# A two-layer convolution network on parity grids: convolutions in 64x64 pieces of the array, two row tiles at a time

## The reference

```python
def odefunc(t, y):
    h = jax.nn.relu(_group_norm(y, gn1_w, gn1_b))
    h = _concat_conv(t, h, conv1_w, conv1_b)      # 3x3, pad 1, an input channel of the constant t in front
    h = jax.nn.relu(_group_norm(h, gn2_w, gn2_b))
    h = _concat_conv(t, h, conv2_w, conv2_b)
    return _group_norm(h, gn3_w, gn3_b)

x = x + dct2(_gn(x))                              # 2-D DCT of each 112x112 channel
y = _gn(x)
for k in range(6): y = y + (1/6) * odefunc(k/6, y)
return x + y                                      # x: 16 images, 32 channels, 112 x 112, float32
```

## Time and profile before

| | |
|---|---|
| median of 3 runs | 3935.17 us (3934.33 to 3935.84) |
| profiled execution, its span | 3928.6 us |
| PE busy, share of the span | 3592.0 us, 91% |
| PEld | 2039.1 us, 52% |
| DVE | 3342.3 us, 85% |
| ACT | 2079.6 us, 53% |
| POOL | 929.9 us, 24% |
| mean granted clock of TensorE | 0.970 |

### The profile page before, as it was taken

One profiled execution on the slowest core, in us unless ns is written; L12 is line 12 of the kernel. 1 busy time (PEld: TensorE's weight loads), 2 busy tenths in 40 slices (PEclk: granted clock), 3 DMA queues, 4 the chain that ended last, 5 costly groups with the idle time before them and its releaser, 6 DMA issues.

```text
span 3928.6 us, 70526 instructions
## 1 busy us (share of the span) xinstructions
PE 3592.0 (91%) x21844; PEld 2039.1 (52%) x21844; DVE 3342.3 (85%) x7423; ACT 2079.6 (53%) x3169; POOL 929.9 (24%) x1589
## 2 busy tenths in 40 slices
PE   3699999999999999999999999999999999999995
PEld 3455554555555555555555555555555555554553
DVE  7688888888888888888888888888888888888885
ACT  0455565555655556555565545655555555655553
POOL 4022212222122221222212231123211322111211
PEclk7899999999999999999999999999999999999998
DMA  3300033113032130311312113311133112231013
GB/s 79 74 17 16 22 45 84 41 60 70 11 84 62 61 58 10 94 63 41 58 42 83 41 41 58 76 49 41 41 58 84 41 41 62 37 83 49 25 41 99
DMA packets 366284, 210.26 MB, mean 54 GB/s; under 512 B 351104, under 2 KB 351472, under 8 KB 364016
## 3 DMA queue, kind: packets, MB, share of 16 engines
q1 hardware_dynamic: 366064, 207.66, 21.2%
HBM read 104.88 MB, written 77.07 MB: 46 GB/s over the span
## 4 chain that ended last, share of the span: by engine, by line
issue 39%; PE 34%; DVE 14%; POOL 10%; ACT 2%; POOLq 1%; DMA 1%; DVEq 0%; SPq 0%; ACTq 0%
PE cps L1246 30%; POOL xn L516 3%; POOL small L479 3%; DVE hb L973 2%; POOL m L513 2%; POOL xn L521 2%; PE xps L1320 2%; DVE hb L976 2%; ACT z L620 2%; DVE bnt L889 1%; POOL hb L496 1%; DVE bnt L896 1%; DVE small L951 1%; DVE bn L1000 1%; DVE ha L976 1%
## 5 line engine op out<-in xcount | busy, mean ns | idle before, releaser
L1246 PE MATMUL cps<-ha,w 128*128 128x399 f16 (+1 forms) x9216 | 1737.6, 342 | 69.7 <-DVE ha L976 64.5
L1246 PE MATMUL cps<-hb,w 128*128 128x448 f16 x8064 | 1645.0, 360 | 0.0
L608 ACT ACTIVATE z<-cps,bias_now 128x448 f32<-128x448 f32 (+2 forms) x1440 | 875.8, 610 | 1128.3 <-PE cps L1246 1100.9
L1246 PEld LDWEIGHTS cps<-ha,w 128*128 128x128 f16 x9216 | 861.0, 99 | 693.6 <-ACT z L608 61.1
L1246 PEld LDWEIGHTS cps<-hb,w 128*128 128x128 f16 x8064 | 748.9, 100 | 678.8 <-issue 41.5
L479 POOL TENSOR_TENSOR small<-small,half 128x1 f32<-128x1 f32 x304 | 190.3, 626 | 2135.6 <-DVE small L942 2133.8
L496 POOL MEMSET hb<- 64x28 f16 (+2 forms) x1152 | 320.5, 278 | 784.6 <-DVE hb L976 666.2
L889 DVE BATCH_NORM_STATS2 bnt<-z 128x6 f32<-128x448 f32 x672 | 413.1, 621 | 94.7 <-ACT z L608 94.7
L620 ACT ACTIVATE z<-z,small 128x798 f32<-128x798 f32 (+1 forms) x384 | 405.8, 1057 | 120.5 <-DVE small L951 120.5
L982 DVE SCALAR_TENSOR_TENSOR y<-z,small,y 128x784 f32<-128x784 f32 x384 | 457.4, 1245 | 6.7
L896 DVE BATCH_NORM_STATS2 bnt<-z 128x6 f32<-128x385 f32 (+1 forms) x768 | 411.4, 546 | 56.9 <-ACT z L608 50.4
(11 more groups left out here) (135 smaller groups left out, 2352.4 us busy)
## 6 DMA issues: line engine op xcount, KB each, us to landing
xa<-x_dram SPq DMA_DIRECT2D x64, 392.0 KB, 7.9
y<-xa SPq DMA_DIRECT2D x16, 1568.0 KB, 7.7
y_dram<-y SPq DMA_DIRECT2D x64, 392.0 KB, 7.1
xs<-in_x_dram SPq DMA_DIRECT2D x31, 784.0 KB, 8.7
x_dram<-x1s SPq DMA_DIRECT2D x30, 784.0 KB, 5.3
fin<-y_dram SPq DMA_DIRECT2D x30, 784.0 KB, 7.8
fin<-x_dram SPq DMA_DIRECT2D x28, 784.0 KB, 8.3
out_dram<-fin SPq DMA_DIRECT2D x28, 784.0 KB, 3.3
```

What stands on the lines that cost most here:

```text
L608: nc.scalar.activation(z[slot][:, r0 * width:(r0 + r) * width], cps[i % BANKS][:, 0:r * width], ACT.Identity, bias=bias_now[:, conv:conv + ...
L1246: return pe.matmul(ps, w[:, tap, wl, :], h[:, hl, r0 + a:r0 + a + r, b:b + width], start=(n == 0), stop=(n == len(products) - 1))
```

## The change

The column parities are no longer shifted between the convolutions: both keep 56 columns, while rows still go from 56 to 57 and back. For columns a 3x3 kernel then has one tap between equal parities and two between different ones (`taps`). Partitions 0 to 63 hold one column parity and 64 to 127 the other, and each product becomes a 64x64 piece from one half of the partitions (`hin`) to one half of the outputs (`hout`).

A pair of row tiles, P from rows of the upper half and Q from rows 28 further down, is convolved together. For rows 28 to 55 the state is stored with its column parities swapped. So the pieces that cross parities in P run between other halves than those of Q, and a round has four pieces on four different quarters of the array, with two banks. X phases have 12 rounds, Y phases 6; `PHASES` orders the four pairs of a convolution. Six banks (three pairs) are used, and the rims' products are 64x64 pieces too.

- ScalarE evacuates pairs of 784 elements per partition (`evacuate`), 4 instead of 7 or 8, with an extra row in convolution 1; it writes the hi part of the hb split itself by a second activation (`activate`); it normalises the half image for the DCT in 16 instructions (`normalise_half`) and copies the rim weights of the step (`set_bias`).
- VectorE loses the hb casts and the rim statistics, takes statistics of 392 elements (`pair_stats`), and takes over `last_add`.
- GpSimd loses `zero_rim`, `centre_half`, `scale_half` and `last_add`. It gets `wrap_rows` (copies the first row of hb to below the last, and zeroes the first, two partition ranges) and `seam` (copies two rows of ha between halves where the swap lies).
- The orders of ScalarE, VectorE and TensorE's small products are written anew for four pairs per phase. Weights shrink to three column taps; state loads and stores go in eight DMAs of half the size instead of four.

```diff
-                products = [(tap, wl, hl) for wl, hl in ((0, 0), (0, 1), (1, 0)) for tap in range(4)]
-                    return pe.matmul(ps, w[:, tap, wl, :], h[:, hl, r0 + a:r0 + a + r, b:b + width],
-                                     start=(n == 0), stop=(n == len(products) - 1))
+PHASES = (("X", 0), ("X", 1), ("Y", 0), ("X", 2), ("Y", 1), ("X", 3), ("Y", 2), ("Y", 3))
+PAIR_BANKS = ((0, 1, 2, 0), (1, 2, 0, 1), (2, 0, 1, 2), (2, 0, 1, 2))
+                taps = {(0, 0): ((1, 0),), (1, 1): ((1, 0),), (1, 0): ((0, -1), (2, 0)), (0, 1): ((0, 0), (2, 1))}
+                def piece(at, first, rows, idx, hin, hout, ix, ox, n):
+                    kinds = [(wl, hl, tap, a) for wl, hl in ((0, 0), (0, 1), (1, 0)) for tap in taps[ix, ox]
+                             for a in range(2)]
+                    wl, hl, (kx, dj), a = kinds[n]
+                    off = (first + idx + a) * P + 1 + dj
+                    src = h[hin * 64:(hin + 1) * 64, hl, off:off + rows * P].rearrange("p (i j) -> p i j", j=P)
+                    dst = cps[hout * 64:(hout + 1) * 64, at:at + rows * NA].rearrange("p (i j) -> p i j", j=NA)
+                    return pe.matmul(dst, w[hin * 64:(hin + 1) * 64, kx, a, wl, :], src[:, :, 0:NA],
+                                     start=(what == "X" and n == 0), stop=(what == "Y" and n == len(kinds) - 1))
+                rounds = 12 if what == "X" else 6
+                for n in range(rounds):
+                    if n in between:
+                        between[n]()
+                    if n == 0:
+                        ready()
...
+                    if what == "X":
+                        p_piece(1, 0, n)
+                        p_piece(0, 1, n)
+                        q_piece(0, 0, n)
+                        last = q_piece(1, 1, n)
+                    else:
+                        p_piece(0, 0, n)
+                        p_piece(1, 1, n)
+                        q_piece(1, 0, n)
+                        last = q_piece(0, 1, n)
```

TensorE, a step's small products (phases 0 to 3; a place is a phase of `PHASES` and a round):

```diff
+                between = {(1, 6): lambda: statistics_of(Z1, 0)}
...
+                between = {(1, 6): lambda: statistics_of(Z1, 1)}
...
+                between = {(1, 6): lambda: statistics_of(Z2, 0)}
...
+                elif kind != LAST:
+                    between[7, 0] = lambda: statistics_of(Y, 0)
...
+                between = {(0, 0): lambda: statistics_of(Z2, 1)}
+                if kind == MID:
+                    for b in range(2):
+                        between[1 + 2 * b, 0] = lambda b=b: rows_of(b)
+                        between[2 + 2 * b, 0] = lambda b=b: dct_columns(b, NBATCH * hn + b, dps)
+                    def state_then_rows():
+                        statistics_of(Y, 1)
+                        rows_of(2)
+                    between[5, 0] = state_then_rows
```

ScalarE, phases 0 and 1, and phase 2:

```diff
+                    evacuate(slot, conv, phase, 0, c)
+                    act.wait_ge(post_done, posted(Z1, other))
+                    activate(other, Z1, 0)
+                    activate(other, Z1, 1)
+                    evacuate(slot, conv, phase, 1, c)
+                    activate(other, Z1, 2)
+                    evacuate(slot, conv, phase, 2, c)
+                    activate(other, Z1, 3)
+                    evacuate(slot, conv, phase, 3, c)
...
+                if kind == MID:
+                    normalise_half(hn)
+                evacuate(1, 1, 2, 0, c)
...
+                    squares(0, 0)
+                    squares(0, 1)
+                    evacuate(1, 1, 2, 1, c)
+                    squares(0, 2)
+                    squares(0, 3)
+                    evacuate(1, 1, 2, 2, c)
+                    evacuate(1, 1, 2, 3, c)
+                    act.wait_ge(post_done, posted(Y, 0))
+                    for k in range(NP):
+                        activate(0, Y, k)
```

VectorE, phase 2 and the start of phase 3 (`updated` waits for the statistics, aggregates, gets the coefficients and updates the state; in phase 3 a split part stands between aggregation and coefficients):

```diff
+                    split_for(3, 0)
+                    split_for(3, 1)
+                    stats_of(2, 2)
+                    stats_of(2, 3)
...
+                updated(1, 1, lambda: split_for(3, 3))
```

More of the change, by code:

```diff
@@ L577, in _ @@
+                seam(0, conv_at(g, s, 3), fixes + 2, pows)
+                pows = rsqrt_of(Z2, 1)
+                if kind != FIVE:
+                    pows = rsqrt_of(Y, 1)
+                seam(1, conv_at(g, s, 4), fixes + 3, pows)
+                if kind == FOUR:
+                    rsqrt_of(IZ, 0)
             with pool.Fori(0, GROUPS - 1) as g:
@@ new lines, in step @@
+                split_for(2, 0)
+                split_for(2, 1)
+                stats_of(1, 1)
+                if kind == MID:
+                    half_post(hn, stats_before(g, s, kind) + STATS[MID].index((X0, 0)))
+                split_for(2, 2)
+                if kind == FIVE:
+                    post_of(IY, 0)
+                if kind == FOUR:
+                    start_stats(0, g + 1, (0, 1))
+                split_for(2, 3)
+                if kind == MID:
+                    with dve.If(g > 0):
+                        last_add(g * HALVES + s)
@@ L1267, in needs, with pair_tiles @@
-            def needs(conv, k):
-                rows = (TILES1, TILES2)[conv]
-                parts = (PARTS_A, PARTS_B)[conv]
-                last = offsets(rows)[k] + rows[k] + (0 if conv == 0 else 1)
-                last = min(last, sum(parts))
-                return next(p + 1 for p in range(NP) if offsets(parts)[p] + parts[p] >= last)
-            def tile(slot, conv, k, i, n, t, ready, base, between=()):
-                if k == 0 or needs(conv, k) > needs(conv, k - 1):
-                    pe.wait_ge(ready, base + needs(conv, k))
-                if not (isinstance(n, int) and n + i < BANKS):
-                    pe.wait_ge(evac_done, n + i - BANKS + 1)
-                conv_tile(slot, conv, k, i, t, between)
+            def pair_tiles(conv, k):
+                if conv == 0:
+                    first = (0, R + 1) if k == 0 else (R * k + 1, R)
+                    return (*first, R * k + 1 + HALF, R, 1)
+                return (R * k, R, R * k + HALF, R, 0)
@@ L1367, in statistics_of @@
                     statistics(slot, what, stats_before(g, s, kind) + STATS[kind].index((what, slot)), wait, value)
-                def among(*places):
-                    return {(k, m): (lambda e=event: statistics_of(*e)) for k, m, event in places}
-                i = 8
-                between = among((2, {MID: 1, FOUR: 1, FIVE: 10}.get(kind, 6), (Z1, 0)))
-                if kind == FIVE:
-                    between.update(among((7, 0, (IZ, 1))))
-                for k in range(8):
-                    tile(1, 0, k, i, n, s, lo_done, parts - NP, between)
-                    i += 1
@@ L1383, in step @@
+                between = {(1, 6): lambda: statistics_of(Z1, 1)}
                 if kind == MID:
[L1384 removed]
+                    between[3, 0] = lambda: half_mean(hn, stats_before(g, s, kind) + STATS[MID].index((X0, 0)))
                 if kind == FIVE:
[L1386 to L1389 removed]
@@ L1391, in step @@
-                between = among((1, 9 if kind == FIVE else 3, (Z2, 0)))
-                if kind not in (FIVE, LAST):
-                    between.update(among((4, 9, (Y, 0))))
-                elif kind == FIVE:
-                    between.update(among((4, 0, (IY, 1))))
-                for k in range(7):
-                    tile(1, 1, k, i, n, s, rim_zero, rim + NP, between)
-                    i += 1
+                    between[5, 0] = lambda: statistics_of(IY, 0)
+                convolve(0, 1, 1, conv_at(g, s, 1), sets + 1, between)
```

920 lines of the change are left out of this document (510 added, 410 removed).

## The result

The changed kernel takes 4397.7 us (median; 4391.8 to 4404.2), the kernel before 3935.5 us beside it: ratio 1.117, 95% interval 1.116 to 1.119. It is 11.7% slower, where 7% faster was forecast; 4398 lies above the range that I gave (3440 to 4120), too.

What follows compares the result with a forecast made beforehand. With no engine full any more, queue order was taken to decide: start 172, seven groups 3066, last group 370, tail 34 make 3642, plus 6.6 outside the span: 3650 us, 7% below; range 3440 to 4120.

Steps and rivals of the forecast that it cites:

- Rounds of 170 ns, loads hidden: TensorE's convolutions: four 64x64 pieces run together in 170 ns, their four weight loads hidden under the stream.
- weight loads queue: Slower rival, between a round's pieces: four loads queue, 225 ns per round, 4055 us in all; chance 0.28.
- less overlap: Slower rival: pieces run in twos, 340 ns a round, TensorE bound again, sum 5350 us; chance 0.16.
- TensorE's part of the sum: Each convolution: 72 rounds of 0.170 us plus 0.8 us of rims, 13.1 us instead of 16.8.
- VectorE 59 us, ScalarE about 54 us in a MID step: Work per step with a half image's DCT: VectorE 59 us, ScalarE about 54 us instead of 42.4.
- The standing behind GpSimd: VectorE operations slowed beside GpSimd's long passes: about 8 us per MID step, expected to go.
- The walk: Queue orders followed through one MID step's four phases, stalls included: 75.5 us.
- eight DCT batches: TensorE's DCT products in a MID step: eight batches at 0.8 us, 6.4 us, as in the kernel before.
- 43.4: no stall: Phase 2: squares end at 43.0 us, the state's product stands at 43.4, so TensorE waits 0.
- evacuation of the last pair 4 to 5 us after its pieces: Sign of being right: ScalarE evacuates a convolution's last pair 4 to 5 us after TensorE finishes it.
- The clock: TensorE products at half clock after the stalls in phase 1 and ahead of phase 3: 1.7 us each.
- FOUR and FIVE: The two steps of each group after its four MID steps: 70 us and 66 us.

Runs made afterwards that it cites:

- b1_nopool: Kernel before, with GpSimd's centring and scaling of the half image moved to ScalarE and its last add to VectorE: 3833.8 us, ratio 0.974.
- e10_flat: Changed kernel with TensorE's loops over the MID steps of a group and over the last group's steps written out: 4329.2 us, ratio 1.100.
- e2_fill: Changed kernel with idle 64x64 pieces on TensorE, read by nobody, ahead of three statistics products of each step: 4155.0 us, ratio 1.056.
- e1_late: Changed kernel with the small statistics products placed later between TensorE's pieces, nothing else: 4298.2 us, ratio 1.093.
- e4_order: e1_late with phase 3's product later still and VectorE's split parts, last add and statistics in another order: 4044.9 us, ratio 1.028.
- e6_all: e4_order with the sixteen normalisations split into two parts and the second hb activation taken back to a VectorE cast: 4006.1 us, ratio 1.018.
- e8_fill: e6_all with idle 64x64 pieces on TensorE in three of its waits: 3922.5 us, ratio 0.995.
- e11_fillflat: e8_fill with TensorE's loops over MID steps written out: 3806.6 us, ratio 0.968.
- e12_best: e11_fillflat with image 1's squares together, its state's product earlier, and eight normalisations ahead of phase 2's squares: 3800.8 us, ratio 0.966.

## Why the prediction was wrong, step by step

*Rounds of 170 ns, loads hidden*: right. 169 ns is the median. The loads of four different quarters do not add up. The rivals "weight loads queue" and "less overlap" fall, although the first named a time (4055) nearer to the one measured. TensorE's part of the sum, 13.1 us a convolution, holds: phase 0 in the step shown (1601.4 to 1617.5) takes 16.1 us with a wait of 2.9 in it.

*VectorE 59 us, ScalarE about 54 us in a MID step*: right, 59.45 and 53.05, the second with some luck: its terms as written add up to 50 to 53 us, and the sixteen normalisations were taken at 0.25 us; they took 0.38 from start to start (6.05 for sixteen) and 0.47 each. The line through 448 and 798 columns did not hold at 112. The last add, 1.8: 1.78. The standing behind GpSimd, 8 us: b1_nopool shows 8.5.

*The walk*: this is where it failed. The terms of a MID step, forecast against measured:

| term | forecast | kernel after |
|---|---|---|
| wait at the product of phase 1 | 3.7 | 5.0 |
| wait at the product of phase 2 | 0 | 5.1 |
| wait ahead of phase 3 | 7.6 | 8.0 |
| wait in phase 0 for split part 2 | 0 | 2.9 |
| rounds at half clock | 3.4 | 5.0 in 31 rounds; 5.7 with those that hold rim pieces |
| eight DCT batches | 6.4 | 7.7 |
| jump back, three MID steps of four | 0 | 2.5 in the mean, by e10_flat |

The measured waits are from piece to piece. Added up, they miss by 15 to 16 us, and the gap between 75.5 and 91.5 (mean of four) is 16.0. Over the span: the start took 189.7 instead of 172, 18 us more; the seven groups 3721.6 (189.7 to 3911.3) instead of 7 x 438 = 3066, 656 more; what follows them 490.7 instead of 370 + 34, 87 more. Their sum, 760, is the span of 4402.0 less the 3642 forecast for it; from median to forecast it is 748.

The row of the DCT had its cause in the change too. From the first of eight products to the next convolution piece it is 0.97 us in the kernel after (median of 196 batches), between 64x64 pieces, and 0.79 before (224 batches), between 128x128 products; the two small statistics products take 0.31 instead of 0.14 us. I had carried the old price over for the first and had none for the second. Timeline of TensorE at full clock:

```profile
1598.18 1.04 PE L1477 MATMUL dps<-dct,xn 112*112 112x112 f32 x8
1599.15 0.53 PE L1369 MATMUL cps<-ha,w 64*64 64x392 f16 x8
```

The step that failed is "43.4: no stall". I had walked the coefficients of phase 2 to the updates and squares, and asked only whether the state's product would wait. But the statistics product of the same chain stands at (1, 6), three us into phase 2, and I had evacuation 3 at 33.1 against a start of 31: even by my own numbers it would have waited about 1 us. Read from the trace, the other 4 are three: evacuation 3 ended 3.5 us into the phase instead of 2.1; the last add, which I had costed at 1.8 us and put into a sum, stands ahead of these very statistics (1551.52 against 1553.22 above); and the statistics of both last pairs stand behind it, 1.97 us where I had walked one pair's. No run moves the last add alone. This wait, 5.1 us where the walk has 0, is the largest single miss of a MID step, a third of the 16. The same with phase 0: split part 2, counted in the sum, stands behind the aggregation (aggregation 1604.00, subtraction 1605.17 to 1606.15, TensorE's next piece 1606.49). Sum and walk used the same terms, but in the walk I had queued them only on ScalarE.

And a wait that I had not thought of as such feeds itself: while TensorE stands, evacuation 0 of the next convolution, which ScalarE has in its queue ahead of the activations, cannot run. In phase 1 the coefficients were there at 1538.1, ScalarE idled 8.4 us in all and took evacuation 0 at 1540.54, the activations behind it at 1541.35. The prediction's last check, "evacuation of the last pair 4 to 5 us after its pieces", looked at the wrong end of that queue.

*The clock*: the mechanism was there, the size was not. Two waits with 1.7 us of slow products behind each, 3.4 us; there were three with slow rounds behind them, 31 in the MID step shown, and a fourth wait, 2.9 us, without. e2_fill puts a price on it, 243 us of the kernel's 4398.

*The jump*: no term at all. It is 69 us of the kernel after, 116 where little else waits.

The shares, as the runs show them one after the other (in another order they would be others: the clock was worth 243 us first and 84 later): order of TensorE's and VectorE's queues 353 us (e1_late, e4_order), hb cast and normalising 39 (e6_all against e4_order; 109 for the cast alone on the kernel after), clock 84 on top of that (e8_fill), jump 116 (e11_fillflat), the rest of the order 6, inside the noise. Together 597 of 748. In the mean e12_best's MID steps take 77.2 us, 1.7 above the forecast's 75.5 (46 us in all), its steps of the last group 69.9 (8 us). FOUR and FIVE, 75.8 and 71.7 against 70 and 66, are 80 us of what is left, the start 15. FOUR stays open: its chain was never walked, only set by a few words, and no run bears on it. Of FIVE the traces show more. Behind it stands the jump back of the whole group, which no run wrote out. Timeline of TensorE in e12_best, at the start of the fourth group:

```profile
1539.53 2.83 PE L1379 MATMUL cps<-ha,w 64*64 64x448 f16 x30 [6.47 <-issue]
```

At the six group ends with this jump TensorE idles 2.8 to 7.4 us in e12_best and 6.3 to 7.5 in the kernel after; at the seventh, where it runs straight on, 1.0 and 1.2. The view of the kernel after names ScalarE's bias and rim weights as releasers, but those are the ones of the next phase, and at three of the six ends in e12_best the pieces start over 4 us ahead of them. The seventh FIVE takes 66.8 us in e12_best, the other six 68.8 to 75.2, so with the jump gone the forecast's 66 would nearly hold. That is read from traces; the run that would show it is a group written out. Open too is how much of e12_best's filling costs anything: it was not run without it.

The rival on the slow side named a slower TensorE. The time came out on that side by another mechanism: a faster engine in front of unchanged chains, with more work queued in them.

## What to carry to other kernels

When the leading engine gets faster, the cover of the other chains shrinks by as much: walk every queue in its order with the new cover, and ask of each item standing ahead of a chain (an add, a split part, an evacuation that itself waits for the stalled engine) whether it is in it. A sum per engine that comes out right to 1% (59.45 against 59) says nothing of that. Work without a deadline goes behind chains, not into them: with the split parts put ahead of theirs that was 253 us here, over a third of the 710 us of streaming that the change took away.

Look for the part of a change that pays alone: taking GpSimd's two long passes and the last add away from VectorE's side was worth 102 us in the old kernel, though it added 6 us of work per MID step to ScalarE. And count an engine's instructions per loop: compare the wait at a jump with that at a place where the same step is reached straight on.

## What the runs showed of the hardware

A jump back in TensorE's loop of a MID step (some 1300 products and as many weight loads) costs 3.0 to 3.8 us of idle time without a releaser in the trace; written out, the same pieces follow at once. At the jump back of a whole group TensorE idles 6.3 to 7.5 us in the kernel after and 2.8 to 7.4 in e12_best; no run wrote that one out. The kernel before, whose step has 477 products, shows no such wait, and its instruction queue moved 1.61 MB against 8.93 (8.32 in e10_flat, where more instructions exist and most are passed once). That the loop's instructions are fetched again is what these numbers suggest, not what they show; at which size of loop it sets in, no run shows either.

Four 64x64 pieces of 392 columns in different quarters run in 169 ns together, like one 128x128 product, with four 64-column weight loads of 0.11 us each hidden, though the loads' sum is more than twice the round. The Trainium skill, "TensorEngine Tiling (Array Packing)", Restrictions, says that column tiling switches fast weight load off; no run here shows whether it was off. At the rate of the Trainium skill, "TensorE: Matmul & The Clock Gate", section LDWEIGHTS, the four loads would be an estimated 213 ns one after the other. The rounds are shorter than that, so the loads did not go one after the other at that rate.

TensorE kept at work with pieces whose results nobody reads mostly keeps 2.4 GHz through waits of 5 to 8 us: mean clock 0.845 without, 0.956 with them, and 5.5% less time.

A batch of other products between 64x64 pieces costs more than between 128x128 products, 0.97 for 0.79 us of eight 112x112 products; why, no run shows.

One-column operations of VectorE take 0.22 us in the mean with GpSimd's long passes gone and 1.63 with them, updates of 784 elements 1.03 and 1.40 (b1_nopool against the earlier trace rows).
